# Moving the first half of P·V and the row sums ahead of the v projections in a graph attention kernel

## The reference

```python
h = relu(layernorm(x))
A = einsum('od,bdn->bon', adj, h); C = einsum('od,bdn->bon', adj, h) + b[None, :, None]
x = x + max(relu(A[:, :, None, :] + (C - A)[:, :, :, None]), axis=-1)
h = relu(layernorm(x))
qkv = (h @ w_qkv).reshape(b, n, 3, 8, 32).transpose(2, 0, 3, 1, 4)
q, k, v = qkv[0], qkv[1], qkv[2]
attn = einsum('bhnd,bhmd->bhnm', q, k) * scale
attn = softmax(where(adj == 0, -inf, attn), axis=-1)
o = einsum('bhnm,bhmd->bhnd', attn, v).transpose(0, 2, 1, 3).reshape(b, n, d)
o = o @ w_proj + b_proj
x = x + o + (o - mu) * rsqrt(var + 1e-5) * gamma + beta
```

## Time and profile before

| | |
|---|---|
| median of 3 runs | 779.43 us (777.5 to 783.04) |
| the profiled execution | 781.43 us, its span 779.7 us |
| PE busy | 724.6 us, 93% of the span |
| DVE busy | 606.4 us, 78% |
| ACT busy | 466.1 us, 60% |
| POOL busy | 395.3 us, 51% |
| DMA | 71.01 MB, mean 91 GB/s |

### The profile page before, as it was taken

The page is one execution under the profiler, slowest core; times in us unless marked ns, Lnnn a source line. Parts: engine busy times, 40 slices in busy tenths (PEclk is TensorE's granted clock), DMA queues, the critical chain, the costliest instruction groups (busy, mean ns, idle before and its releaser), DMA issues.

```text
span 779.7 us, 37319 instructions
## 1 busy us (share of the span) xinstructions
PE 724.6 (93%) x16233; PEld 490.2 (63%) x16233; DVE 606.4 (78%) x1458; ACT 466.1 (60%) x1033; POOL 395.3 (51%) x720
## 2 busy tenths in 40 slices
PE   1789999999999999999999999999999999999851
PEld 0356666666666666666666666666666766666540
DVE  3568888787888888888888888888888888878642
ACT  4456675556666655667666556676665566774420
POOL 4324455554556455554564554545545546454433
PEclk9999999999999999999999999999999999999975
DMA  6333335535544665464455544543455345424222
GB/s 191 104 84 84 59 83 110 111 87 108 70 86 96 112 110 96 99 112 77 77 98 110 111 93 102 111 70 81 102 111 111 87 108 110 84 38 77 29 28 28
DMA packets 102835, 71.01 MB, mean 91 GB/s; under 512 B 68369, under 2 KB 101905, under 8 KB 102161
## 3 DMA queue, kind: packets, MB, share of 16 engines
q1 hardware_dynamic: 85776, 51.85, 26.9%
q0 software_dynamic: 16896, 16.78, 16.7%
HBM read 35.06 MB, written 33.55 MB: 88 GB/s over the span
## 4 chain that ended last, share of the span: by engine, by line
PE 90%; DVE 3%; ACT 2%; issue 2%; DMA 1%; POOL 1%; SPq 0%; DVEq 0%; POOLq 0%
PE a_ps L309 21%; PE sum_ps L427 11%; PE a_ps L321 11%; PE pv_ps L396 8%; PE sum_ps L399 7%; PE sc_ps L375 6%; PE sc_ps L350 6%; PE sc_ps L330 6%; PE a_ps L291 5%; PE sum_ps L424 3%; PE pv_ps L411 2%; PE sc_ps L379 2%; PE sc_ps L356 1%; DVE smax L649 1%; DMA w_sb<-in_L_gnn_w_qkv 1%
## 5 line engine op out<-in xcount | busy, mean ns | idle before, releaser
L542 ACT ACTIVATE p_sb<-sc_ps 128x512 f32<-128x512 f32 x256 | 140.4, 607 | 37.2 <-PE sc_ps L379 37.2
L649 DVE TENSOR_REDUCE smax<-sc_ps 128x4 f32<-128x512 f32 x256 | 157.6, 677 | 1.8 <-PE sc_ps L350 1.8
L834 POOL TENSOR_TENSOR oT_lo<-oT,oT_hi 128x256 f16<-128x256 f32 x128 | 83.4, 672 | 132.1 <-ACT oT_hi L555 132.1
L309 PE MATMUL a_ps<-hT,w_hi 128*128 128x512 f16 x512 | 133.2, 383 | 5.9 <-DMA hT<-h_parts 3.2
L548 ACT ACTIVATE pv_sb<-pv_ps 128x512 f32<-128x512 f32 x64 | 38.2, 597 | 144.6 <-PE sum_ps L399 144.6
L637 DVE TENSOR_TENSOR qk_lo<-a_ps,qk_hi 128x512 f16<-128x512 f32 x128 | 87.4, 683 | 29.7 <-ACT qk_hi L529 29.5
L396 PE MATMUL pv_ps<-p_sb,v_sb 128*32 128x128 f32 x2048 | 104.9, 276 | 1.9 <-ACT pv_sb L548 1.3
L399 PE MATMUL sum_ps<-p_sb,sel_sum 128*32 128x128 f32 x2048 | 103.4, 273 | 0.0
L687 DVE BATCH_NORM_STATS2 st<-o_sb 128x6 f32<-128x256 f32 x128 | 53.6, 420 | 49.5 <-ACT o_sb L561 49.4
L828 POOL TENSOR_TENSOR h_parts<-h_sb,h_parts 128x256 f16<-128x256 f32 x128 | 82.1, 673 | 18.8 <-ACT h_parts L507 18.7
L529 ACT ACTIVATE qk_hi<-a_ps 128x512 f16<-128x512 f32 x128 | 77.4, 604 | 9.4 <-PE a_ps L309 9.3
(11 more groups left out here) (106 smaller groups left out, 1772.7 us busy)
## 6 DMA issues: line engine op xcount, KB each, us to landing
x_sb<-in_x SPq DMA_DIRECT2D x32, 512.0 KB, 5.4
out<-in_x SPq DMA_DIRECT2D x32, 512.0 KB, 5.5
out<-y_sb POOLq DMA_DIRECT2D x32, 512.0 KB, 6.2
w_sb<-in_L_gnn_w_qkv SPq DMA_DIRECT2D x1, 768.0 KB, 6.7
hT<-h_parts SPq DMA_TRANSPOSE x33, 4.6
wp_sb<-in_L_gnn_w_proj SPq DMA_DIRECT2D x1, 256.0 KB, 5.4
gamma_sb<-in_L_gnn_ln_gamma SPq DMA_DIRECT2D x1, 128.0 KB, 5.9
beta_sb<-in_L_gnn_ln_beta SPq DMA_DIRECT2D x1, 128.0 KB, 6.8
```

The costliest lines, as they stand in the source:

```text
L309: mm = nc.tensor.matmul(a_ps[c % 2][:].rearrange("p (b n) -> p b n", b=G), w[:, dc, col:col + P], hT[:, par, part, :, dc], start=(k == 0), ...
L542: nc.scalar.activation(p_sb[:, j, i], sc_ps[i][:], ACT.Exp, scale=SCALE).then_inc(p_ready, 1)
L649: nc.vector.tensor_reduce(smax[:, i, 0, j], sc_ps[i][:], AX.X, ALU.max).then_inc(smax_ready, 1)
L834: nc.gpsimd.tensor_tensor(oT_lo[:, b], oT[:, b], oT_hi[:, b], ALU.subtract).then_inc(olo_ready, 1)
```

## The change

The four `P` units stand behind `S1` and ahead of `V0 V1` on TensorE, and on ScalarE the copy `A0` of their result stands ahead of `V0`. No instruction is added, removed or altered.

```diff
-            ORDER = ("Q0 Y0 Y1 Y2 Y3 N0 E0 Q1 R0 Q2 K0 S0 R1 O0 Q3 O1 L0 N1 E1 O2 L1 O3 K1 S1 V0 V1 P0 P1 P2 P3 M0").split()
+            ORDER = ("Q0 Y0 Y1 Y2 Y3 N0 E0 Q1 R0 Q2 K0 S0 R1 O0 Q3 O1 L0 N1 E1 O2 L1 O3 K1 S1 P0 P1 P2 P3 V0 V1 M0").split()
...
-            ORDER = ("Y0 Q0 E0 E1 E2 Q1 E3 C0 Q2 R0 R1 R2 O0 C1 R3 H0 Q3 H1 H2 H3 O1 E4 E5 O2 E6 E7 O3 V0 L0 A0 M0 V1").split()
+            ORDER = ("Y0 Q0 E0 E1 E2 Q1 E3 C0 Q2 R0 R1 R2 O0 C1 R3 H0 Q3 H1 H2 H3 O1 E4 E5 O2 E6 E7 O3 A0 V0 L0 M0 V1").split()
```

## The result

The new order takes 787.0 us (median of 6 runs, 784.7 to 791.49), the old one 780.4 us beside it (6 runs). The ratio is 1.0091, with a 95% interval of 1.0057 to 1.0125: slower by 0.9%, where 776.3 us and a range of 772.5 to 780.8 us were forecast. The profiled execution took 784.7 us, the shortest of the six, and its span is 782.8 us.

What follows compares the result with a forecast made beforehand. TensorE was taken to bound the kernel, a middle step being its own program of 22.32 us. One tile-shape change less, 31 x 0.10 = 3.1 us, off the median 779.43 gave 776.3 us, range 772.5 to 780.8 us.

Steps and rivals of the forecast that it cites:

- TensorE bounds the kernel and a middle step is its own program: Middle steps: TensorE busy 356.17 of 357 us, 22.32 us a step; reordering pays only by changing what lies between blocks.
- One change of shape less, 0.10 us a step: TensorE's step end: two tile-shape changes instead of three, 0.10 us gained in 31 steps, 3.1 us; chance 0.70.
- a rival of its own: M0's weight load slips under the last v matmuls, the step gains 0.18 us: 773.3 us; chance 0.07.
- S1 to P0, the border without a row: Border from scores 32*128 to P·V 128*32, not in the profile: taken as 0.10 us, bounded by 0 and 0.2 us.
- What M0 waits for: M0 waits for VectorE's U0, done at 349.81; of 0.18 us of room the change leaves 0.08 us.
- its own sign that VectorE sets the step: A sign of being wrong: M0 standing 0.05 us behind U0.
- The cap: M0's room of 0.18 us behind U0 limits what a step can gain.
- The moved blocks have what they wait for: P0 has 0.70 us of room; ScalarE's copy of v's first half ends 0.66 us ahead of Q0.
- The instructions and their lengths are the same, so nothing else changes: TensorE's step end: reordering leaves instructions and lengths as they are; only the number of shape changes differs.
- No DMA is issued by either moved step, so queues do not matter: The queues of SP and POOL keep their order, and what they wait for is far off; no cost counted.
- The ends: TensorE's two waits for ScalarE's copy of P·V, 1.3 us together; step 32's goes, counted as nothing, at most 0.55 us.
- The slower one: Q0 waits for ScalarE's copy of v's first half, 0.54 us late in 31 steps: 793 us; chance 0.04.

Runs made afterwards that it cites:

- even_100_after: New kernel with exactly 1024 TensorE instructions a step and 174 put in at the start, M0 always at place 100 of its 256-instruction block: 774.05 us.
- even_100_before: Old order with exactly 1024 TensorE instructions a step, M0 always at place 100 of its 256-instruction block: 778.53 us.
- after_shift_84: New kernel with only 84 matmul and weight load instructions put into TensorE's idle time at the start: 777.31 us, ratio 0.9961.
- after_no_dma: New kernel with SP's transposes, loads and copies of x replaced by tiny transfers from step 3 (loads: group 6) on: 777.1 us.
- act_order_only: Old kernel with only ScalarE's new order (A0 ahead of V0), TensorE's order as before: 818.67 us.
- even_254_after: New kernel with exactly 1024 TensorE instructions a step and 72 put in at the start, M0 always at place 254 of its 256-instruction block: 811.24 us.
- after_no_transposes: New kernel with the DMA transposes of h replaced by 256-byte copies from step 3 on: 787.97 us.
- even_254_no_transposes: New order, 1024 TensorE instructions a step, M0 always at place 254 of its block, only SP's transposes left out: 805.13 us.

## Why the prediction was wrong

- *TensorE bounds the kernel and a middle step is its own program.* True for the orders, the semaphores and the borders; false for the instructions themselves. The earlier trace rows is a window of quiet steps only. The window from 78 to 194 us, shown above, had 2.6 us of idle time with no engine as its cause, and the prediction left it aside.
- *One change of shape less, 0.10 us a step.* Right, and too small: the borders give 0.10 us (0.31 less 0.09 and 0.12), and M0's load under the last v matmuls another 0.06, which I had given as a rival of its own with a chance of 0.07. Together the step is 0.15 us shorter, 4.5 us in 30 steps (even_100_after against even_100_before), where 3.1 us were in the sum.
- *S1 to P0, the border without a row.* I took 0.10 us; it is 0.09.
- *What M0 waits for.* U0 ends and M0's weights load 0.05 us behind it (489.35 + 0.17 to 489.57). That is the least that the prediction allowed, and its own sign that VectorE sets the step: counted from the end of S1, U0 ends where it did, and the load comes 0.19 us earlier, so the room of 0.18 us is used up. The cap was right; I had expected 0.08 us to be left.
- *The moved blocks have what they wait for.* Right. The copy of v's first half ends at 489.16, 0.61 us ahead of Q0 at 489.77, where 0.66 was worked out. The views of both:

```profile
488.56 0.60 ACT L522 ACTIVATE v_sb<-a_ps 128x512 f32<-128x512 f32 x1 [0.79 <-PE a_ps L321]
...
489.35 0.17 DVE L653 COPY smax<-smax 128x32 f32<-128x32 f32 x1
```

- *The instructions and their lengths are the same, so nothing else changes.* This is the step that failed. The supply of instructions stood in the sum at nothing, without a reason. The same 64 matmuls of P, with their 64 weight loads, moved 2.7 us forward, into the time in which the next block of instructions is late behind SP's transfers. That is worth 7.0 us more of excess in the profiled run, against a gain of 4.5 us. The shift of the blocks (after_shift_84) took 9.7 us off the median, and leaving out the transfers (after_no_dma) 9.9 us.
- *No DMA is issued by either moved step, so queues do not matter.* True of the data queues. TensorE's instruction stream is a queue too, q8, 1.2% of the DMA engines' time on the page of the kernel before, which I read first.
- *The ends.* Right: the wait of 0.55 us of Y0 in step 32 is gone, and one of 0.8 us is left of two (1.3 us together before). I had counted nothing for it.
- *The rivals.* The slower one named the wrong wait. The 817 us worked out in its way for act_order_only held to 2 us, which shows how little a well-priced rival helps if the list is short of one. That the loss of the change itself stayed within 1%, where the prediction had put a chance of 0.92, is luck: no case of it but the slower rival gave a loss at all, and the size of this one hangs on where the blocks begin. even_254_after, at 811.24 us, lies 4% over the kernel before.

The Trainium skill has a rule that bears on this and that I did not weigh: the page Runtime: NRT & Kernel Launch, section Instruction fetch mechanics, says that instructions are refilled in 16 KiB blocks, 256 instructions, over a DMA queue while the current block executes. The trace agrees with the block, 2.10 MB in 128 packets. The same section calls the cost of a border mostly hidden; in even_100_after it was, and elsewhere it was up to 3.5 us in a step (after_no_transposes) and 37 us between the medians of even_100_after and even_254_after.

## What to carry to other kernels

Where one engine is the bound and its program is unrolled, count its instructions, not only its time: a stretch of many short instructions behind a slow stretch cost nothing here at places 100 and 254, and the same stretch ahead of it ran dry at 254 while large transfers kept the DMA engines busy. An "issue" wait in the middle of a run of matmuls that wait for nothing is the sign, and the proof is its place: count the records, and see whether these waits lie at one place modulo 256. Before an order is judged by its time, shift the stream by some tens of instructions or make the count of a step a multiple of 256: the same order measured 774, 777, 787 and 811 us by little else (the first and the last with seven waits fewer in a step), where the order itself is worth 4.5 us.

## What was not expected of the hardware

- A block of 256 instructions of TensorE comes as one packet of q8. In quiet time it starts about 0.6 us behind the point at which the count puts the request (taken as 60 instructions ahead of the running one, an estimate from the traces), in busy time 1.5 to 3.5 us. In the stalled step TensorE went on 2.3 us behind the packet's start, and 2.2 to 2.5 us behind it in nearly every stall of even_254_after.
- The stalls have two modes under one program: 0.25 us a step or about 2.2 us a step. In even_254_after the longer one held from step 13 to step 30, in even_254_no_transposes for four steps (26 to 29) and then ended. What tips a run from one into the other stays open.
- The float32 transpose M0 takes 0.10 us up to Q0 behind matmuls of its own tile shape, and 0.16 us behind the 128\*32 sums. In the first case its weights load 0.10 us ahead of it, in the second 0.01 us.
